# One core, a modulated layer and a small mixture of experts: the order of the first loads, and who forms the rest of x

## What is computed

```python
# first layer: a weight matrix per batch, mixed from 8 by y = cond_8[b], under a mask
masked_w = weight * mask[None, :, :]
w_bot = jnp.einsum('bg,got->bot', y, masked_w)
x = x + jnp.einsum('bnt,bot->bno', x, w_bot) + bias
# second layer: the top 2 of 8 experts by softmax(cond_8), plus a shared one
out = sum over the two of  w_e * gemma_mlp(x, gate_e, up_e, down_e)
out = out + gemma_mlp(x, shared_gate, shared_up, shared_down)      # inner width 1024
x = x + out
```

## Time and profile before

| | |
|---|---|
| median of 3 runs | 411.5 us |
| the profiled execution | 411.14 us |
| its span, first to last instruction | 409.1 us |
| granted TensorE clock, mean | 1.000 |
| TensorE busy | 404.4 us, 99% |
| VectorE, ScalarE, GpSimd busy | 301.7, 254.1, 313.3 us |
| start of `first_gate_up` on TensorE | 14.56 us |

### The profile page before, as it was taken

One profiled execution on the slowest core, in us unless ns is written; L12 is line 12 of the kernel. 1 busy time (PEld: TensorE's weight loads), 2 busy tenths in 40 slices (PEclk: granted clock), 3 DMA queues, 4 the chain that ended last, 5 costly groups with the idle time before them and its releaser, 6 DMA issues.

```text
span 409.1 us, 7375 instructions
## 1 busy us (share of the span) xinstructions
PE 404.4 (99%) x2199; PEld 351.0 (86%) x2199; DVE 301.7 (74%) x518; ACT 254.1 (62%) x483; POOL 313.3 (77%) x322
## 2 busy tenths in 40 slices
PE   8999999999999999999999999999999999999997
PEld 5788888888888888888888888888888888889886
DVE  5788876567769888765777889857687767677784
ACT  4887776666564677664646666757455556666541
POOL 1699999999729689999625969999670977999630
PEclk9999999999999999999999999999999999999999
DMA  8653332323200623323010262223200042241201
GB/s 300 211 149 91 100 121 88 103 79 104 77 2 4 199 56 109 104 101 103 28 26 1 56 198 79 77 77 108 72 26 26 2 144 62 77 136 47 53 1 51
DMA packets 18894, 35.21 MB, mean 86 GB/s; under 512 B 2098, under 2 KB 2610, under 8 KB 18866
## 3 DMA queue, kind: packets, MB, share of 16 engines
q1 hardware_dynamic: 18576, 34.61, 27.5%
q10 hardware_dynamic: 290, 0.26, 0.2%
HBM read 32.77 MB, written 2.10 MB: 85 GB/s over the span
## 4 chain that ended last, share of the span: by engine, by line
PE 97%; DVE 1%; ACT 0%; issue 0%; POOL 0%; DVEq 0%; POOLq 0%
PE o_ps L582 16%; PE g_ps L528 11%; PE u_ps L527 11%; PE u_ps L528 11%; PE u_ps L531 11%; PE g_ps L527 10%; PE g_ps L531 10%; PE p_ps L582 9%; PE l_ps L482 2%; PE p_ps L590 2%; PE p_ps L591 1%; PE u_ps L432 1%; PE o_ps L631 0%; PE p_ps L447 0%; DVE t_raw L1000 0%; DVE out_sb L1157 0%
## 5 line engine op out<-in xcount | busy, mean ns | idle before, releaser
L1268 POOL TENSOR_TENSOR eg_lo<-raw_g,eg_hi 128x512 fp32r<-128x512 f32 x64 | 91.6, 1452 | 10.4 <-ACT eg_hi L747 10.4
L780 ACT ACTIVATE gelu<-g_ps 128x512 f32<-128x512 f32 x95 | 56.9, 599 | 53.2 <-PE g_ps L531 51.8
L1076 DVE SCALAR_TENSOR_TENSOR u_ps<-gelu,route_cur,u_ps 128x512 f32<-128x512 f32 x64 | 48.1, 752 | 50.9 <-PE u_ps L531 47.7
L1112 DVE TENSOR_TENSOR h_both<-t_raw,h_both 128x1024 fp32r<-128x1024 f32 x46 | 76.4, 1661 | 0.5 <-ACT h_both L813 0.5
L1310 POOL TENSOR_TENSOR ed_lo<-s_raw,ed_hi 128x512 fp32r<-128x512 f32 x30 | 51.7, 1722 | 0.0
L800 ACT CAST h_both<-u_ps 128x256 fp32r<-128x256 f32 x46 | 17.2, 373 | 54.8 <-DVE t_raw L1091 33.4
L528 PE MATMUL g_ps<-x_hi,eg_lo 128*128 128x512 f32 (+1 forms) x128 | 50.2, 392 | 0.0
L527 PE MATMUL g_ps<-x_hi,eg_hi 128*128 128x512 f32 (+1 forms) x128 | 50.0, 391 | 0.0
L527 PE MATMUL u_ps<-x_hi,eg_hi 128*128 128x512 f32 (+1 forms) x128 | 49.8, 389 | 0.0
L528 PE MATMUL u_ps<-x_hi,eg_lo 128*128 128x512 f32 (+1 forms) x128 | 49.8, 389 | 0.0
L813 ACT CAST h_both<-t_raw 128x1024 fp32r<-128x1024 f32 x46 | 47.9, 1041 | 0.5 <-DVE t_raw L1098 0.5
(11 more groups left out here) (232 smaller groups left out, 1048.6 us busy)
## 6 DMA issues: line engine op xcount, KB each, us to landing
raw_g<-experts SPq DMA_DIRECT2D x64, 256.0 KB, 2.8
raw_d<-experts SPq DMA_DIRECT2D x32, 256.0 KB, 2.7
raw_g<-shared SPq DMA_DIRECT2D x8, 256.0 KB, 5.5
l_raw<-l_w SPq DMA_DIRECT2D x3, 512.0 KB, 5.6
x_in<-xT SPq DMA_DIRECT2D x6, 256.0 KB, 3.7
outT<-out_sb SPq DMA_DIRECT2D x6, 256.0 KB, 3.0
raw_d<-shared SPq DMA_DIRECT2D x4, 256.0 KB, 2.9
x_in<-xT SPq DMA_DIRECT2D x1, 512.0 KB, 4.3
```

What stands on the lines that cost most here:

```text
L780: act.activation(gelu[:, s % 2], l0_ps if at_first(b) and s == 1 else g_ps, ACT.Gelu_apprx_tanh).then_inc(gelu_done, 1)
L1076: dve.scalar_tensor_tensor(u_ps[:, s % 2], gelu[:, s % 2], route_cur[:, k:k + 1], u_ps[:, s % 2], ALU.mult, ALU.mult).then_inc(h_done, 1)
L1112: dve.tensor_tensor(h_lo[:, at], t_raw[:], h_hi[:, at].bitcast(F32), ALU.subtract).then_inc(t_lo_done, 1)
L1268: pool.tensor_tensor(eg_lo[:, j % RING], raw_g[:, j % RAW_G], eg_hi[:, j % RING].bitcast(F32), ALU.subtract).then_inc(gu_lo_done, 1)
```

## The change

On SP the loads take a new order: half 0's two loads of weights, the mask, half 0 of x, half 1's three loads of weights, and last half 1 of x; x is loaded in two DMAs in place of one, each with its own semaphore. g=6 of half 0 is combined on VectorE and no longer mixed on TensorE. The `x_lo` of x's half 0 is made by GpSimd, ahead of its wait for the mask; that of half 1 stays on VectorE, behind the masks of half 1. TensorE's and ScalarE's orders follow the new arrivals. Four of the route's small steps move behind `first_x1_lo`, two behind the second combine. In `first_gate_up` the second and third products change places.

```diff
-        DIAGS = (2, 3, 6, 7, 5)
+        DIAGS = (2, 3, 7, 5)
@@ SP
             load_l0(0, 0)
-            load_x_0()
             load_l0(0, 1)
+            sp.dma_start(mask[:], l0_mask).then_inc(mask_in, 16)
+            load_x_half(0, 0)
             load_l0(1, 0)
-            sp.dma_start(mask[:], l0_mask).then_inc(mask_in, 16)
             for i in range(2):
                 load_l0_last(i)
+            load_x_half(0, 1)
             shared_weights()
@@ TensorE, first_layer_0
+                pass_x(0)
+                mix_l0(1, 2, first=True)
                 pe.wait_ge(first_hi_done, 1)
-                for th in range(HH):
-                    first_layer_part(l0_hi, 0, th, x_hi)
+                first_layer_part(l0_hi, 0, 0, x_hi)
+                mix_l0(1, 3)
+                pass_x_rest(0)
+                first_layer_part(l0_hi, 0, 0, x_lo)
+                pe.wait_ge(first_lo_done, 1)
+                first_layer_part(l0_lo, 0, 0, x_hi)
+                mix_l0(1, 5)
                 mix_l0(1, 7, last=True)
-                for th in range(HH):
-                    first_layer_part(l0_hi, 0, th, x_lo)
-                pe.wait_ge(first_lo_done, 1)
-                for th in range(HH):
-                    first_layer_part(l0_lo, 0, th, x_hi, last=(th == HH - 1))
-                for th in range(HH):
-                    pe.wait_ge(first_hi_done, 2 + th)
-                    for x in (x_hi, x_lo):
-                        first_layer_part(l0_hi, 1, th, x)
+                pass_x(1)
+                first_layer_part(l0_hi, 0, 1, x_hi)
+                first_layer_part(l0_lo, 0, 1, x_hi)
+                pe.wait_ge(first_hi_done, 2)
+                first_layer_part(l0_hi, 1, 0, x_hi)
+                pe.wait_ge(x_lo_done, 2)
+                first_layer_part(l0_hi, 0, 1, x_lo, last=True)
+                first_layer_part(l0_hi, 1, 0, x_lo)
+                pass_x_rest(1)
+                pe.wait_ge(first_hi_done, 3)
+                for x in (x_hi, x_lo):
+                    first_layer_part(l0_hi, 1, 1, x)
                 for th in range(HH):
                     pe.wait_ge(first_lo_done, 2 + th)
                     first_layer_part(l0_lo, 1, th, x_hi, last=(th == HH - 1))
@@ TensorE, first_gate_up
-                    for ps, off, hi_done in ((g_ps, GATE, part_hi_done), (u_ps[:, 0], UP, gu_hi_done)):
+                    for ps, off, hi_done, lo_done in ((g_ps, GATE, part_hi_done, part_lo_done), (u_ps[:, 0], UP, gu_hi_done, gu_lo_done)):
                         at = off + hh * P
                         pe.wait_ge(hi_done, 1)
                         pe.matmul(ps, w_hi[:, at:at + P], x1_at(x1_hi, 0, hh), start=(hh == 0), stop=False)
-                    for ps, off, lo_done in ((g_ps, GATE, part_lo_done), (u_ps[:, 0], UP, gu_lo_done)):
-                        at = off + hh * P
                         pe.wait_ge(lo_done, 1)
@@ TensorE, the opening
             mix_l0(0, 2, first=True)
             mix_l0(0, 3)
-            pass_x(0)
-            keep_warm(1)
-            pass_x(1)
-            mix_l0(0, 6)
             mix_l0(0, 7, last=True)
-            for hh in range(HH):
-                pass_x_rest(hh)
-            mix_l0(1, 2, first=True)
-            for g in (3, 5):
-                mix_l0(1, g)
+            keep_warm(2)
             first_layer_0()
@@ ScalarE
-            for hh in range(HH):
-                split_x(0, hh)
+            split_x(0, 0)
+            split_l0_0()
             scale_first()
-            split_l0_0()
             act.activation(gelu[:, 0, 0:8], shifted[:, 0], ACT.Gelu_apprx_tanh)
-            split_gate(0)
+            split_x(0, 1)
             for th in range(HH):
                 split_l0_1(th)
+            split_gate(0)
+            first_x1_hi(0)
             split_up(0)
-            first_x1_hi(0)
@@ VectorE
             route_sums()
-            route_pair()
-            route_weigh()
             combine_0(0, 0)
             combine_0(0, 1)
-            for hh in range(HH):
-                first_x_lo(hh)
+            route_probs()
             combine_0(0, 4)
             combine_0(0, 5)
+            combine_0(0, 6)
             add_mixed_0()
             apply_mask_0()
+            split_l0_0()
             combine_0(1, 1)
             combine_0(1, 4)
-            split_l0_0()
             combine_0(1, 6)
             for th in range(HH):
                 add_mixed_1(th)
                 apply_mask_1(th)
+            first_x_lo_1()
             for th in range(HH):
                 split_l0_1(th)
             for oh in range(HH):
                 first_x1_lo(oh)
+            route_pair()
+            route_weigh()
             route_index()
```

More of the change, by code:

```diff
@@ L282, in load_l0_last @@
                 sp.dma_start(l0_raw[:, 1, at], l0_w[1, 1, :, bass.ds(2 * i * D, 2 * D)].rearrange("p (g d) -> p g d", d=D)).then_inc(l0_in[3 + i], 16)
-            def load_x_0():
-                sp.dma_start(x_in[:], xT[0]).then_inc(x_loaded[0], 16)
             def shared_gu(c):
@@ L695, in split_x @@
             def split_x(b, hh):
[L696 to L699, removed]
+                act.wait_ge(x_loaded[hh], 16 * b + 16)
                 if hh == 0 and not at_first(b):
@@ L968, in route_sums, with route_probs @@
                 dve.reciprocal(exp_rsum[:], exp_sum[:]).then_inc(weighed, 1)
+            def route_probs():
                 dve.wait_ge(weighed, 2)
@@ L998, in combine_0 @@
                     else:
-                        dve.wait_ge(first_mixed, {1: 1, 4: 2, 5: 3}[g] if oh == 0 else {4: 5, 6: 6}[g])
+                        dve.wait_ge(first_mixed, {1: 1, 4: 2, 5: 3, 6: 4}[g] if oh == 0 else {4: 6, 6: 7}[g])
                     dve.scalar_tensor_tensor(acc, w, cond_all[:, 0, g:g + 1], acc, ALU.mult, ALU.add).then_inc(first_mixed, 1)
             def add_mixed_0():
-                dve.wait_ge(first_mixed, 4)
+                dve.wait_ge(first_mixed, 5)
                 dve.wait_ge(mixed, 1)
@@ L1013, in add_mixed_1 @@
                 at = slice(D + th * P, D + (th + 1) * P)
-                dve.wait_ge(first_mixed, 7)
+                dve.wait_ge(first_mixed, 8)
                 dve.wait_ge(mixed, 2)
@@ L1030, in split_l0_1, with first_x_lo_1 @@
                 dve.tensor_tensor(l0_lo[:, at], l0_first[:, at], l0_hi[:, at].bitcast(F32), ALU.subtract).then_inc(first_lo_done, 1)
-            def first_x_lo(hh):
-                dve.wait_ge(x_hi_done, hh + 1)
-                dve.tensor_tensor(x_lo[:, hh], x_in[:, hh], x_hi[:, hh].bitcast(F32), ALU.subtract).then_inc(x_lo_done, 1)
+            def first_x_lo_1():
+                dve.wait_ge(x_hi_done, 2)
+                dve.wait_ge(x_lo_done, 1)
+                dve.tensor_tensor(x_lo[:, 1], x_in[:, 1], x_hi[:, 1].bitcast(F32), ALU.subtract).then_inc(x_lo_done, 1)
             def first_x1_lo(oh):
```

## The result

| | before | changed |
|---|---|---|
| median | 411.44 us (6 runs, 410.92 to 411.69) | 414.66 us (6 runs, 413.45 to 415.42) |
| ratio | | 1.0078, 95% interval 1.0065 to 1.009 |
| profiled execution, its span | 411.14, 409.1 | 415.42, 412.9 |
| mean granted clock of TensorE | 1.000 | 0.996 |
| `first_gate_up` | 14.56 | 18.17 |

The change makes the kernel 3.2 us slower. 412.1 was forecast, with 413.3 as the upper end of the range. The last two lines say where the time is: in the opening, 3.6 us of the 3.8 between the two profiled spans. Behind it 0.2 us are new, with a gap of 0.1 in `first_gate_up`.

A forecast was written before the change was run, and what follows sets the result against it. The opening was taken to bound the edit's worth, through `first_gate_up` at 14.56: add 11.63, masks 12.68, `x_lo` 13.44, seven passes and restart, 15.15. So 411.14 + 0.6 = 411.74, plus 0.36 to the median: 412.1, range 411.3 to 413.3.

The forecast's parts named there:

- I place each by the bytes ahead of it.: Opening loads: landing times follow bytes queued ahead; x half 0 at 7.4 to 7.5, half 1's weights at 8.6.
- TensorE's pace: TensorE in the opening: a mix costs 0.86 or 0.43 us by clock level, the change coming near 8.6.
- Rival C: TensorE's opening: new idle places may delay the high pace, +1.25 us on top, 413.35; chance 0.08.
- The chain from half 1's first mix to `first_gate_up`: Opening, from half 1's first mix at 8.65 to `first_gate_up` at 15.15: 6.50 us.
- four mixes and passes: TensorE from 8.65: four mixes and four passes stand ahead of the end of half 1's mix; add at 11.63.
- `x_lo` 0.69: VectorE behind both masks of half 1: forming the rest of x's half 1 takes 0.69 us, on the path.
- seven passes behind the wait: TensorE after waiting for x's second rest: seven passes at 0.23, 1.6 us, before `first_gate_up`.
- The add of half 0: VectorE in the opening: half 0's weights come earlier, so its add starts at 7.53, against 9.29.
- The route steps: Four small steps, 0.8 us, moved before VectorE's product at 17.91: hidden in 1.12 us of idle time.
- the late up rest: GpSimd's first up rest, near 15.8, wanted in `first_gate_up` at 15.85: just covered, 0.1 us if not.
- Rival A: VectorE/GpSimd lock: GpSimd wins the race at 8.1, delaying the mask; `first_gate_up` at 16.2, +1.65, 413.15; chance 0.22.
- Rivals B and D: B: half 1's weights land 0.3 to 0.6 earlier, 411.5; D: no wait on x's second rest, 411.5; together 0.12.

The follow-up runs named there:

- d1: Changed kernel with x loaded whole as third load, the mask behind it and no separate load of half 1: 414.56 us, ratio 1.0071.
- d2: Kernel before with x loaded as two halves in a row, second and third in the queue: 412.87 us, ratio 1.0025.
- i1: Kernel before without four of its idle products on TensorE, loads untouched: 411.6 us, ratio 1.0012.
- w2: Changed kernel with five idle products on TensorE where there are two, loads untouched: 412.79 us, ratio 1.0031.
- p1: Changed kernel with mask behind x's half 0, four idle products for two, and half 1's `x_lo` formed before VectorE's add: 412.32 us, ratio 1.0026.
- a_again: The changed kernel once more, unedited, beside its variants: 414.88 us, ratio 1.0088.

## Why the prediction was wrong

The forecast was 412.1, the time 414.66, outside the range. Of the 3.0 us between the forecast 15.15 for `first_gate_up` and the 18.17 of the profile, 1.37 are the later start of half 1's first mix (10.02 for 8.65) and 1.65 the stretch behind it (8.15 for 6.50). The 1.65 lie wholly between that mix and the add of half 1 (4.64 for 2.98); from the add on it is 3.51 for 3.52.

**The step that failed first: "I place each by the bytes ahead of it."** Half 1's weights were to land "at 8.6 as before", with as many bytes ahead of them. They land at 9.46 to 9.91 in four profiles of this order, x's half 0 at 8.15 to 8.66 and not 7.4 to 7.5. The rate of the queue was taken as given, at some 400 GB/s, while the change put the mask (257 KB) and half of x (256 KB) ahead of them, where all of x, one load of 512 KB, had stood. d1, d2 and the rates of the other profiles lay the slow stretch on x's halves; that the mask adds to it is not shown. A part is chance: the same order of loads had these weights 0.4 apart in the kernel before (8.66, and 9.08 in i1). In all, half 1's first mix is 0.9 to 1.4 us late.

**The step that failed next: TensorE's pace.** Rival C named idle places "near 8.5, 12.2, 13.0" and gave 0.08, "up to 8.5 it is as busy as before". With x's half at 8.66 it was not: it stood from 7.9 to 9.4. The price was 1.25 for two mixes and two passes; it was 1.65, with parts of three mixes and some passes. The chance was too low because it hung on the first step, and the two were treated as independent: a late x is what makes TensorE stand. w2 shows the step by itself: with the stand filled and the loads as they were, the ratio goes from 1.0088 to 1.0031. Rival C's time, 413.35, was made without the late weights, so it fell short too.

**What held.** The chain from half 1's first mix to `first_gate_up`, worked out as 6.50, measured 6.51 to 6.53 in each of five profiles at full clock; so the terms in it (four mixes and passes, masks 1.05, `x_lo` 0.69, seven passes behind the wait) are sized right, and p1 shows 0.34 of it directly. The add of half 0 came at 7.32 where 7.53 stood (7.12 to 7.45 in the variants), the mask at 7.89 for 8.06. The route steps and the late up rest cost at most 0.2. Rival A, the lock, did not decide: x came too late for a race at 8.1. What the lock did instead is what the sum held: `split_l0_0` took 1.30 and not 0.42, beside the path. Rivals B and D stayed away.

A row that I did not weigh may have pointed the right way: in the profile of before, x's half loads of later batches take 3.7 us to land and weights of the same size 2.8 (medians). What those loads queue behind was not looked at.

## What to carry to other kernels

A load that is moved in the opening need not arrive at its bytes divided by the old rate: look at what size and shape of transfer now stands in front, and price the new order with a slower queue (here half the rate for 2.5 us) as one end of the range. Where a transfer comes late, ask at once which engine stands still for it, and whether that is TensorE: the two losses come together, here 1.4 and 1.6 us, and filling the wait with idle products won back about 2.1 us of 3.3 in the medians. Before trusting such a filler, look at the end of the program too: with four products more a fetch of instructions stood among the final stores, and the profile's end was 1.5 us longer.

## What was not expected of the hardware

- The granted clock was 1.00 until near 11, 0.50 from 11 to 14.4, with TensorE standing from 7.9 to 9.4: the fall came 1.5 us after work had started again. The Trainium skill (TensorE: Matmul & The Clock Gate, "What's actually happening") has activity release a throttled default state, and the point of that release vary from run to run. Here it is the fall that differed between two profiles of one program: at 11 in one and not at all in the other (a_again), though TensorE also stood 1.54 us in the one and 0.84 in the other.
- Early in the execution the record says granted clock 1.00 while the pace is that of 1.2 GHz (up to 11 us in d2, up to 15 in d1). The pace of the records, and not that column, told the level there. So there are two ways to lose time to the pace, a fall after it has risen and a late rise; why it rose late in d1 and d2 was not tested.
- One order of loads, four profiles: x's half 0 cast at 6.64, 6.89, 7.29 and 8.19 us.
